# Attention's loads of keys, queries and values in smaller transfers, spread over sixteen rows of a head

## What is computed

```python
q = (x @ Wq + bq).reshape(1, B * N, H, hd)
kv = (cond @ Wkv + bkv).reshape(1, -1, 2, H, hd)
...
q = _fq_sym(q, axis=-1)
k = _fq_sym(k, axis=-1)
v = _fq_sym(v, axis=2)
attn = jnp.einsum('bhqd,bhkd->bhqk', q, k)
attn = jax.nn.softmax(attn.astype(jnp.float32), axis=-1)
attn = _fq_unsigned(attn, axis=-1)
out = jnp.einsum('bhqk,bhkd->bhqd', attn, v)
out = jnp.transpose(out, (0, 2, 1, 3)).reshape(B, N, C)
return out @ Wp + bp
```

## Time and profile before

| | us |
|---|---|
| runs of the kernel, median (lowest to highest) | 2685.33 (2680.43 to 2685.69) |
| the profiled execution | 2687.95 |
| its span, first to last instruction | 2686.2 |
| VectorE busy | 2478.9 |
| TensorE busy (matmuls) | 2212.1 |
| ScalarE busy | 2009.7 |
| GpSimd busy | 1443.9 |

### The profile page before, as it was taken

The page is one execution under the profiler, slowest core; times in us unless marked ns, Lnnn a source line. Parts: engine busy times, 40 slices in busy tenths (PEclk is TensorE's granted clock), DMA queues, the critical chain, the costliest instruction groups (busy, mean ns, idle before and its releaser), DMA issues. The chain is left out here.

```text
span 2686.2 us, 53043 instructions
## 1 busy us (share of the span) xinstructions
PE 2212.1 (82%) x20020; PEld 1181.0 (44%) x20020; DVE 2478.9 (92%) x3614; ACT 2009.7 (75%) x1862; POOL 1443.9 (54%) x1879
## 2 busy tenths in 40 slices
PE   8999999788887787777888888787787777868886
PEld 4454445344444444444444444444444444433433
DVE  6998758699999999999999999999999999957997
ACT  4454444389888888888888888888888888855655
POOL 2432322155767666676666667676666767551001
PEclk9999999877778877887677777878878888779999
DMA  7566454699999999999999999999999999990000
GB/s 234 145 154 143 97 135 101 150 184 182 193 193 203 202 179 201 199 189 184 191 205 173 205 201 186 191 198 203 178 199 202 183 199 177 175 226 19 16 20 24
DMA packets 1406612, 445.65 MB, mean 166 GB/s; under 512 B 1337444, under 2 KB 1377892, under 8 KB 1405256
## 3 DMA queue, kind: packets, MB, share of 16 engines
q1 hardware_dynamic: 1391816, 403.47, 80.4%
q10 hardware_dynamic: 14624, 40.06, 5.9%
HBM read 80.66 MB, written 44.02 MB: 46 GB/s over the span
## 5 line engine op out<-in xcount | busy, mean ns | idle before, releaser
L913 DVE TENSOR_SCALAR_CACHE_REDUCE arena<-a_ps_s 128x1281 f32<-128x1281 f32 (+1 forms) x1280 | 1824.3, 1488 | 23.7 <-PE a_ps_s L853 16.6
L960 ACT ACTIVATE arena<-arena,a_bias,a_row_scale 128x3328 uint8<-128x3328 f32 (+1 forms) x512 | 1560.5, 3049 | 241.9 <-POOL a_bias L1019 241.3
L853 PE MATMUL a_ps_s<-arena,q_rep 96*128 96x512 bf16 (+2 forms) x3840 | 1201.6, 434 | 345.6 <-DVE arena L913 313.9
L853 PEld LDWEIGHTS a_ps_s<-arena,q_rep 96*128 (+1 forms) x3840 | 310.7, 108 | 782.8 <-DVE arena L913 456.5
L866 PEld LDWEIGHTS a_ps_o<-v_head,a_nT 128*128 128x128 f16 x13056 | 524.3, 102 | 263.6 <-issue 148.5
L866 PE MATMUL a_ps_o<-v_head,a_nT 128*128 128x32 f16 x13056 | 514.1, 182 | 28.9 <-POOL a_nT L1027 26.2
L1026 POOL CAST a_nT<-arena 128x1664 int16<-128x1664 uint8 x256 | 401.8, 1569 | 211.1 <-DMA arena<-arena 205.7
L1027 POOL CAST a_nT<-arena 128x1664 int16<-128x1664 uint8 x256 | 402.8, 1573 | 0.0
L1015 POOL TENSOR_SCALAR a_row_max<-a_row_max,a_part_max 128x1 f32<-128x1 f32 x256 | 92.1, 360 | 348.4 <-DVE arena L913 339.8
L376 POOL TENSOR_TENSOR p_rest<-p_kq,p_parts 128x512 f32<-128x512 f32 (+1 forms) x51 | 74.9, 1469 | 286.0 <-ACT p_parts L486 286.0
L406 PE MATMUL p_ps_k<-p_wkv,p_ctxT 128*128 128x512 f32 (+1 forms) x408 | 185.3, 597 | 0.0
(11 more groups left out here) (150 smaller groups left out, 1936.0 us busy)
## 6 DMA issues: line engine op xcount, KB each, us to landing
k_parts_transposed<-arena SPq DMA_DIRECT2D x25, 768.0 KB, 6.5
values<-arena SPq DMA_DIRECT2D x51, 256.0 KB, 6.5
p_ctx<-in_ctx_dram SPq DMA_DIRECT2D x25, 512.0 KB, 5.0
arena<-k_parts_transposed ACTq DMA_DIRECT2D x42, 240.1 KB, 4.2
arena<-in_L_ffn_W_dram SPq DMA_DIRECT2D x8, 1024.0 KB, 8.1
arena<-k_parts_transposed ACTq DMA_DIRECT2D x42, 160.1 KB, 3.7
a_late_v<-values ACTq DMA_DIRECT2D x21, 288.0 KB, 4.0
a_late_v<-values ACTq DMA_DIRECT2D x21, 256.0 KB, 3.7
```

Source lines behind the costliest of these rows:

```text
L853: last = nc.tensor.matmul(ps_s[:, b, n0:n0 + w], q, k_parts[0:3 * HD, slot, start[c] + n0:start[c] + n0 + w], start=True, stop=True)
L913: nc.vector.tensor_scalar(s_row[:, u, start[c]:start[c] + size[c]], ps_s[:, (u + c) % 2, 0:size[c]], 1.0, None, ALU.mult, ALU.max, accum_o ...
L960: nc.scalar.activation(out, s_row[:, u, keys_of_half[half]], ACT.Exp, scale=row_scale[:, u, 0:1], bias=bias[:, u:u + 1], accum_out=zsum[:, ...
```

## The change

The key loads of the next head become twelve transfers of a quarter of the key columns of one part each, in rows 0 to 11; the three query loads stand in rows 12, 13 and 14. A head then has 15 loads, and TensorE's wait counts 15 times 16. Each part of the values is loaded in two halves; the twelve halves are issued every second row, from row 5 of the even head to row 11 of the odd head. Each part has a semaphore of its own, and GpSimd waits for a part at its own step instead of for all six ahead of the first. The loads of the first group ahead of row 0 come in twelve halves too.

```diff
--- before.py
+++ after.py
@@ -766,7 +766,7 @@
     SUMS_AT, INVERT_AT, SCALE_AT = 2, 7, 15
 
     ROUND_AT, ROUND_PARTS = 3, 6
-    RELOAD_AT = [ROUND_AT + 2 + 2 * part for part in range(ROUND_PARTS - 1)] + [QT - 1]
+    RELOAD_AT = ROUND_AT + 2
 
     FIRST_LOADS = 96
     V_PARTS = {1: (0, 13), 2: (13, 26), 3: (26, 39), 4: (39, KT)}
@@ -808,7 +808,8 @@
         ps_s = ph.ps("ps_s", [P, 2, BUF])
         ps_o = ph.ps("ps_o", [P, 2, BANK])
 
-        late_v_loaded, v_scaled, v_rounded = ph.sem("late_v_loaded"), ph.sem("v_scaled"), ph.sem("v_rounded")
+        v_scaled, v_rounded = ph.sem("v_scaled"), ph.sem("v_rounded")
+        part_loaded = [ph.sem(f"v_part{i}_loaded") for i in range(ROUND_PARTS)]
         scores_ready, scores_taken = ph.sem("scores_ready"), ph.sem("scores_taken")
         three_done = ph.sem("three_done")
         row_max_ready, bias_ready = ph.sem("row_max_ready"), ph.sem("bias_ready")
@@ -878,7 +879,7 @@
             PP = QT // 2
 
             def rows_of_head(h, slot, loaded):
-                pe.wait_ge(head_loaded[slot], FIRST_LOADS if h < 2 else FIRST_LOADS + (loaded - 1) * 144)
+                pe.wait_ge(head_loaded[slot], FIRST_LOADS if h < 2 else FIRST_LOADS + (loaded - 1) * 16 * 15)
                 for i in range(2):
                     for u in range(2):
                         t = 2 * i + u
@@ -930,28 +931,29 @@
         def _(act):
             MIDDLE = start[2]
 
-            def load(h, slot, s, half):
-                keys = slice(0, MIDDLE) if half == 0 else slice(MIDDLE, K)
-                act.dma_start(k_parts[s * HD:(s + 1) * HD, slot, keys],
-                             k_dram[s, ds(h * HD, HD), keys]).then_inc(head_loaded[slot], 16)
-                if half == 0:
-                    return
-                act.dma_start(q_rep[s * HD:(s + 1) * HD, slot, :],
-                             q_dram[ds(h * HD, HD), :]).then_inc(head_loaded[slot], 16)
-
-            def next_head(h, slot, step):
-
-                if step == 0:
+            def next_head(h, slot, t):
+
+                if t == 0:
                     act.wait_ge(scores_ready, (h - 1) * (QT * NCH))
-                if step < 6:
-                    load(h, slot, step // 2, step % 2)
-
-            def load_late_values(group, part):
-
-                after_first(act, v_rounded, ((group - 1) * GROUP - 1) * ROUND_PARTS + part + 1 if group > 1 else 0)
-                tiles = slice(part * KT // ROUND_PARTS, (part + 1) * KT // ROUND_PARTS)
+                if t < 12:
+                    s, quarter = t // 4, t % 4
+                    keys = slice(quarter * K // 4, (quarter + 1) * K // 4)
+                    act.dma_start(k_parts[s * HD:(s + 1) * HD, slot, keys],
+                                 k_dram[s, h * HD:(h + 1) * HD, keys]).then_inc(head_loaded[slot], 16)
+                elif t < 15:
+                    s = t - 12
+                    act.dma_start(q_rep[s * HD:(s + 1) * HD, slot, :],
+                                 q_dram[h * HD:(h + 1) * HD, :]).then_inc(head_loaded[slot], 16)
+
+            def load_late_values(group, part, half):
+
+                if group > 1 and half == 0:
+                    act.wait_ge(v_rounded, ((group - 1) * GROUP - 1) * ROUND_PARTS + part + 1)
+                first, end = part * KT // ROUND_PARTS, (part + 1) * KT // ROUND_PARTS
+                middle = (first + end) // 2
+                tiles = slice(first, middle) if half == 0 else slice(middle, end)
                 act.dma_start(late_v[:, tiles, :].rearrange("p t c -> p (t c)"),
-                              v_dram[group, :, tiles, :].rearrange("p t c -> p (t c)")).then_inc(late_v_loaded, 16)
+                              v_dram[group, :, tiles, :].rearrange("p t c -> p (t c)")).then_inc(part_loaded[part], 16)
 
             def exponent(row, u):
                 act.wait_ge(bias_ready, row + 1)
@@ -976,18 +978,21 @@
                     exponent(row, t % 2)
                     if not (isinstance(row, int) and row < TAKE_LAG):
                         take_output(row - TAKE_LAG, t % 2)
-                    if h >= 1 and h % GROUP == 0 and h // GROUP + 1 < H // GROUP and t in RELOAD_AT:
-                        load_late_values(h // GROUP + 1, RELOAD_AT.index(t))
+
+                    step = (h % GROUP * QT + t - RELOAD_AT) // 2
+                    if t % 2 == RELOAD_AT % 2 and h >= GROUP and h // GROUP + 1 < H // GROUP and 0 <= step < 2 * ROUND_PARTS:
+                        load_late_values(h // GROUP + 1, step // 2, step % 2)
                     if h == 1 and t < C // P:
                         scale_projection(t)
-                    if not last and t < 7 and not (isinstance(h, int) and h == 0):
+                    if not last and t < 15 and not (isinstance(h, int) and h == 0):
                         next_head(h + 1, 1 - slot, t)
 
             later = slice(T // 2, T)
             for s in range(3):
                 act.dma_start(q_rep[s * HD:(s + 1) * HD, 1, later], q_dram[HD:2 * HD, later]).then_inc(late_q_loaded[1], 16)
             for part in range(ROUND_PARTS):
-                load_late_values(1, part)
+                for half in range(2):
+                    load_late_values(1, part, half)
             act.dma_start(wp[:], A.wp.rearrange("(j p) n -> p j n", p=P)).then_inc(wp_loaded, 16)
             for i, dram in enumerate((A.bp, A.ln_w, A.ln_b)):
                 act.dma_start(vectors[:, i, :], dram.partition_broadcast(P)).then_inc(wp_loaded, 16)
@@ -1046,8 +1051,9 @@
                 at_ = n % GROUP * HD
                 tiles = slice(part * KT // ROUND_PARTS, (part + 1) * KT // ROUND_PARTS)
                 some = late_v[:, tiles, at_:at_ + HD]
+                if step % 2 == 0 and n % GROUP == 0:
+                    pool.wait_ge(part_loaded[part], 32 * (n // GROUP + 1))
                 if step == 0:
-                    pool.wait_ge(late_v_loaded, 16 * ROUND_PARTS * (n // GROUP + 1))
                     pool.wait_ge(values_done, (h - 1) * QT)
                 if step % 2 == 0:
                     inverse = inv_v[:, h * HD:(h + 1) * HD].unsqueeze(1).to_broadcast([P, tiles.stop - tiles.start, HD])
```

## The result

The changed kernel takes 2724.36 us in the median of four runs (2722.34 to 2726.92), the kernel before 2683.45 beside it: a ratio of 1.0148, with a 95% interval of 1.0134 to 1.0162. It is 1.5% slower, 41 us. The forecast was 2714 us and slower, 29 us above its own base.

What follows compares the result with a forecast made beforehand. The prediction took VectorE to bound attention; -15 us of stalls gone and +44 us at heads' starts sum to +29 us, 2717 us for the profiled execution and 2714 us in the median, range 2690 to 2738.

Steps and rivals of the forecast that it cites:

- The bound: Attention is VectorE's: only a stall of VectorE or a change of its instructions moves its end; 256 rows take 1848 us.
- The exposed landing: At the starts of heads 2 to 15, row 14's query load lands uncovered: 14 stalls of 3.1 us, +44 us.
- rival 2: At heads' starts, row 14's issue goes out early enough to hide the landing; only the gain is left: 2670 us, chance 0.09.
- 1.63: At a head's end, us from the last query load's issue to VectorE's next row; VectorE's backlog, subtracted from each stall.
- S: At a head's start, time from TensorE's restart to VectorE's start: 1.36 us at the lower clock, about 0.83 at the higher.
- L: At a head's end, time from the last query load's issue to its landing: taken as 3.4 us, between 2.0 and 5.1.
- The gain: VectorE's waits for scores in attention go: between 0 and -15.6 us, taken as -15.
- The reason of the gain: In row 5 of every even head from 4 on, three loads bunch; the lateness reaches VectorE three rows later, 15.6 us together.
- the nearest rows say that 240 KB do no harm: Rows 9 and 11 of even heads issue 256 to 288 KB without a VectorE stall, so some 240 KB per row was judged harmless.
- What was costed at nothing: ScalarE's added issues (some 2.8 us per head), six more value issues ahead of row 0, GpSimd's waits per values part: 0.
- A cheap landing (1): At heads' starts, the lone last query load lands in as little as 2.0 us: 2687 to 2694, say 2691 us, chance 0.12.
- That spreading doesn't help (3): In attention, total traffic makes the lateness, not bunching: the 15 us stay and the boundary adds 44, 2729 us; chance 0.12.

Runs made afterwards that it cites:

- keys_only: The kernel before with only its key loads changed to twelve quarters in rows 0 to 11, queries and values as before: 2673.50 us, ratio 0.9958.
- before_late_q: The kernel before with only its three query loads moved from rows 1, 3 and 5 to rows 12, 13 and 14: 2727.66 us, ratio 1.0155.
- q_one_row_earlier: The changed kernel with its three query loads in rows 11, 12 and 13 instead of 12, 13 and 14: 2672.20 us, ratio 0.9958.
- values_only: The kernel before with only the values' part changed: twelve halves over even and odd head, a semaphore per part: 2689.10 us, ratio 1.0025.

## Why the prediction was right, point by point

**The bound.** Right. Nearly all of the difference in attention, 33.4 us of the 36.8 between its first and last starts, was waits of VectorE, and its instructions kept their 1487 ns. Where the waits were zero, the time was 10 to 11 us below the kernel before, whichever version it was.

**The exposed landing.** Right in place, number and kind. The prediction read from ScalarE's program that the issue in row 14 stands behind the wait for the values of row 12, and from the earlier trace rows that such an issue comes 1.63 us before VectorE's next row. The trace after shows 14 stalls, at the starts of heads 2 to 15 and nowhere else, each behind a load issued 0.04 us after TensorE's last matmul. Its argument against rival 2, that no issue lies earlier in its row than that, held.

**Its size.** The term was sized at 44 us and is 49.0 by the waits, and 52 by the step from 2672.20 to 2724.36. Of the three numbers in the stall, 1.63 was right (1.61 in the mean), S was predicted as 1.36 and is 1.38, with 0.83 and 0.85 at the other clock level. The term that was mis-sized is L: 3.7 us in the mean instead of 3.4. The prediction took the 160 KB row, 3.7, and went 0.3 below it for the smaller load. By the 8 KB load, 0.9 us for 120 KB, those 32 KB are worth 0.25 us, so the step itself was fair; the landings in this place are a little longer than that row says, and no run shows why. L and 0.05 us from the landing to the restart, which the sum left out, make the stall 3.5 instead of 3.1, 14 times 0.4. What is left, 52 less 49, stays open: VectorE's rows take a few us more in sum without a wait that the profile lists, and no experiment here shows the reason.

The formula of the Trainium skill (page "DMA: Bandwidth & Descriptors", section "Anatomy of one DMA", about 2.0 us fixed plus bytes over 436e3) gives an estimate of 2.3 us for this load. That section of the Trainium skill fits it to DMAs issued from GpSimd, and these are issued from ScalarE's queue. The measured 3.7 decides against it here, with DMA engines that are busy for nine tenths or more; the share of its fixed part, most of the time, the trace bears out, with 2.8 us for 8 KB. The same page of the Trainium skill has the rule to issue early and wait late (section "Rules for kernel authors"); this change broke it, and one row of distance was enough to mend it. The Trainium skill's rule to coalesce (same section) was not borne out here: `keys_only` has twice as many and smaller key loads and is faster by 0.42%.

**The gain.** Taken as -15 and measured as -11 (0.9958, with an interval that reaches from 0.9943 to 0.9973). The sum used the 15.6 us of one profiled execution, which took 2687.95 us and lay 4.5 above the median of 2683.45; that it had more of these stalls than most was not looked at, so that this is the cause is not shown; the difference is of this size. The two errors, 8 us on the boundary and 4 on the gain, point the same way and make 41 of the forecast 29.

**The reason of the gain.** Here a step was wrong that didn't show in the sum. The prediction blamed three loads on top of each other in row 5, the values among them. That much the traces bear out: without queries (`before_late_q`) or without the long key load (`keys_only`) the stalls are gone, and where the kernel before has no values in row 5, no stall over 0.45 us follows. But it weighed rows by their bytes, and there the kinds of load decide too: 496 KB of keys and values did no harm, 496 KB with the queries among them did in six rows of 24. The step failed at "the nearest rows say that 240 KB do no harm": rows 9 and 11 of the earlier trace rows's head hold loads of values only, and were no like for loads of another kind.

**What was costed at nothing.** ScalarE's added issues, GpSimd's waits by part and the longer list at the start of attention cost nothing that the waits show: ScalarE still waits 229.6 us for the bias, so it had time to spare, and with the boundary mended no wait of VectorE for scores is left in attention.

**The rivals.** A cheap landing (1) would have needed 2.0 us; even 8 KB take 2.8 in the mean (one of the fourteen took 2.0). The hidden boundary (2) is what `q_one_row_earlier` makes of it, 2672 where the rival said 2670. That spreading doesn't help (3) is refuted by the stalls that went.

## What to carry to other kernels

When a load is moved later to even out the traffic, look for what its issue waits for in its own queue's program, and for what its consumer does last before it asks: if both are the same instruction, the whole landing is exposed, whatever its size, and one step of distance takes all of it back. The landing had a part that a smaller piece didn't shrink, 2.8 of 3.7 us here, so the last piece of a set costs nearly as much as a whole one. And weigh a bunch of transfers by a run that takes one kind away, not by its bytes: here half of the change gave all of the gain, and moving the queries a single row early gives a kernel that beats both, 2672 us.

## What the runs showed that I had not expected

Eight matmuls whose result is thrown away made the kernel some 5 us faster, because TensorE came out of its wait at the upper clock level in nine of fourteen cases and handed over the first scores after 0.85 instead of 1.38 us. A landing beside the stream of transposes is 2.8 us for 8 KB and 3.7 for 128 KB, and still 3.7 for a second 128 KB issued right behind a first. And rows with about the same bytes, some 500 KB, differ in whether the transposes fall behind: the slowest wide issue is 7.60 us in `values_only`, which has the long key load, and 5.23 in `keys_only`, with a key load of shorter runs.
